# Adding both halves of every scan state to memory by accumulating transfers, in a decoder layer on one core

## The reference, cut to what matters

```python
def step(state, inp):
    d, b, c, u = inp
    dA = jnp.exp(d[..., None] * A)
    state = state * dA + (d * u)[..., None] * b[:, None, :]
    y = jnp.einsum('bdn,bn->bd', state, c)
    return (state, y)
...
y = y + D[None, :, None] * x
```

## Time and profile before

| | |
|---|---|
| median of 3 runs | 1617.96 us (1610.71 to 1623.04) |
| the profiled execution | 1609.87 us |
| its span in the profile | 1608.0 us |
| mean granted TensorE clock | 0.936 |
| TensorE busy | 1388.2 us (86%) |
| VectorE busy | 1288.5 us (80%) |
| GpSimd busy | 1137.2 us (71%) |
| ScalarE busy | 1044.1 us (65%) |

### The profile page before, as it was taken

One profiled execution on the slowest core, in us unless ns is written; L12 is line 12 of the kernel. 1 busy time (PEld: TensorE's weight loads), 2 busy tenths in 40 slices (PEclk: granted clock), 3 DMA queues, 4 the chain that ended last, 5 costly groups with the idle time before them and its releaser, 6 DMA issues.

```text
span 1608.0 us, 23140 instructions
## 1 busy us (share of the span) xinstructions
PE 1388.2 (86%) x7536; PEld 1130.4 (70%) x7536; DVE 1288.5 (80%) x2377; ACT 1044.1 (65%) x2411; POOL 1137.2 (71%) x613
## 2 busy tenths in 40 slices
PE   3645789998999999999989899985678998998996
PEld 1213678887878877878978788874456676776784
DVE  4898688998888898888898889897548577486575
ACT  3888366666666766666667667675457567577474
POOL 1345489888889888889988899998576266266263
PEclk8777889999999999999999999999689999999998
DMA  5485636656846666856676765657342122111021
GB/s 162 142 292 217 191 83 171 173 147 165 224 119 172 167 147 174 217 144 146 176 175 168 203 163 119 170 123 191 99 146 79 32 92 75 65 55 66 33 68 60
DMA packets 130314, 225.50 MB, mean 140 GB/s; under 512 B 11705, under 2 KB 61377, under 8 KB 128657
## 3 DMA queue, kind: packets, MB, share of 16 engines
q1 hardware_dynamic: 120400, 188.36, 36.9%
q0 software_dynamic: 9792, 35.66, 14.3%
HBM read 145.99 MB, written 77.99 MB: 139 GB/s over the span
## 4 chain that ended last, share of the span: by engine, by line
DVE 33%; PE 32%; issue 11%; ACT 10%; POOL 8%; DMA 5%; SPq 0%; DVEq 0%; POOLq 0%; ACTq 0%
PE banks L607 7%; PE banks L609 6%; PE banks L608 6%; DVE state L1175 5%; POOL act_buf L1974 5%; DVE negmax L1115 4%; PE banks L1514 3%; PE banks L1515 3%; PE banks L1516 3%; DVE prob L1129 2%; DMA x_lo<-scratch_xs 2%; ACT prob L944 2%; DVE banks L423 1%; DVE state_more L1175 1%; DVE qT_lo L1105 1%
## 5 line engine op out<-in xcount | busy, mean ns | idle before, releaser
L1306 POOL TENSOR_TENSOR state<-state,Cn 128x1024 f32<-128x1024 f32 x100 | 246.2, 2462 | 75.2 <-DVE state L1175 75.1
L1974 POOL TENSOR_TENSOR act_buf<-act_buf,wb 128x512 f32<-128x512 f32 x128 | 165.3, 1293 | 171.0 <-ACT act_buf L1873 169.2
L1281 POOL TENSOR_TENSOR state<-dtu_sb,Bn 128x1024 f32<-128x1024 f32 x103 | 249.6, 2424 | 21.6 <-DMA Bn<-scratch_bc 19.8
L1175 DVE TENSOR_TENSOR_SCAN state<-banks,state 128x512 f32<-128x512 f32 x206 | 249.8, 1213 | 2.6 <-ACT banks L998 2.0
L998 ACT ACTIVATE banks<-dt_sb,negA 128x512 f32<-128x512 f32 x256 | 177.3, 692 | 92.8 <-DVE state L1175 71.3
L607 PE MATMUL banks<-x_hi,w_hi 128*128 128x512 f32 (+1 forms) x512 | 187.3, 366 | 48.8 <-DVE qT_lo L1105 14.9
L609 PE MATMUL banks<-x_hi,w_lo 128*128 128x512 f32 (+1 forms) x512 | 178.7, 349 | 0.0
L608 PE MATMUL banks<-x_lo,w_hi 128*128 128x512 f32 (+1 forms) x512 | 178.5, 349 | 0.0
L607 PEld LDWEIGHTS banks<-x_hi,w_hi 128*128 128x128 f32 x512 | 101.9, 199 | 70.6 <-issue 26.1
L2022 DVE TENSOR_TENSOR hid_lo<-banks,hid_hi 128x512 fp32r<-128x512 f32 x136 | 93.7, 689 | 53.3 <-ACT hid_hi L1885 51.4
L2032 DVE TENSOR_TENSOR banks<-banks,act_buf 128x512 f32<-128x512 f32 x136 | 94.3, 693 | 49.0 <-POOL act_buf L1974 25.5
(11 more groups left out here) (226 smaller groups left out, 4587.4 us busy)
## 6 DMA issues: line engine op xcount, KB each, us to landing
scratch_y<-state POOLq DMA_DIRECT2D x52, 512.0 KB, 5.9
x_hi<-scratch_xs SPq DMA_DIRECT2D x32, 512.0 KB, 5.7
x_lo<-scratch_xs SPq DMA_DIRECT2D x32, 512.0 KB, 9.0
Cn<-scratch_bc SPq DMA_DIRECT2D x64, 256.0 KB, 3.7
Bn<-scratch_bc SPq DMA_DIRECT2D x64, 256.0 KB, 4.1
scratch_acc<-acc_sb SPq DMA_DIRECT2D x64, 256.0 KB, 2.2
wb<-scratch_wT SPq DMA_DIRECT2D x64, 256.0 KB, 3.3
acc_sb<-scratch_acc SPq DMA_DIRECT2D x48, 256.0 KB, 3.1
```

Source lines behind the costliest of these rows:

```text
L1175: nc.vector.tensor_tensor_scan(row, dA[:, :], row, 0.0, ALU.mult, ALU.add) \
L1281: nc.gpsimd.tensor_tensor(ring(k), dtu[:, 2 * h:2 * h + 2, :], Bn[:, state % NB, :].unsqueeze(1).broadcast_to([P, 2, T]), ALU.mult).then_i ...
L1306: nc.gpsimd.tensor_tensor(to, ring(k), Cn[:, state % NB, :].unsqueeze(1).broadcast_to([P, 2, T]), ALU.mult).then_inc(S["gated"], 1)
L1974: nc.gpsimd.tensor_tensor(act_[:, N % 3, :], act_[:, N % 3, :], wb[:, E % 3, :], ALU.mult) \
```

## The change

No half state is summed on chip any more. Every half state, h = 0 and h = 1, is gated in its ring buffer and added to memory by a transfer of its own. A transfer waits, on GpSimd, until the one before it to the same place has landed. The running sum y_sb goes; its room becomes a sixth buffer of the ring. A ring buffer comes free when its transfer has landed. The code that waits for the end of the sums is changed to match.

```diff
-RING = 5
+RING = 6
...
-    y = sb("y_sb", [P, 2, T])
-    st_more = sb("state_more", [P, 1, 2, T])
+    st_more = sb("state_more", [P, 2, 2, T])
...
-        def wait_free(k):
+        def wait_added(k):

             state, h = divmod(k, 2)
-            b, r = divmod(state, NS)
-            if h == 1:
-                pool.wait_ge(S[f"y_added1{state % 2}"], 16 * (state // 2 + 1))
-            elif r == 0:
-                pool.wait_ge(S["gated"], k + 1)
-            else:
-                pool.wait_ge(S["piece_done"], (NS - 1) * b + r)
+            pool.wait_ge(S[f"y_added{h}{state % 2}"], 16 * (state // 2 + 1))
...
             if k >= RING:
-                wait_free(k - RING)
+                wait_added(k - RING)
...
-            to = ring(k)
-            if h == 0 and r == 0:
-                if b > 0:
-                    pool.wait_ge(S["y_added0"], 16 * b)
-                to = y[:, :, :]
-            nc.gpsimd.tensor_tensor(to, ring(k),
+            nc.gpsimd.tensor_tensor(ring(k), ring(k),
                                     Cn[:, state % NB, :].unsqueeze(1).broadcast_to([P, 2, T]),
                                     ALU.mult).then_inc(S["gated"], 1)
-            if h == 0 and r > 0:
-                pool.wait_ge(S["gated"], k + 1)
-                nc.gpsimd.tensor_tensor(y[:, :, :], y[:, :, :], ring(k), ALU.add) \
-                    .then_inc(S["piece_done"], 1)
             if k + 3 < NDRIVE:
                 drive(k + 3)
-            if h == 1:
-                pool.wait_ge(S["gated"], k + 1)
-                if r > 0:
-                    wait_free(k - 2)
-                nc.gpsimd.dma_start(d["y"][b][:, 2 * T:4 * T],
-                                    ring(k).rearrange("p c t -> p (c t)"), accum_op=ALU.add) \
-                    .then_inc(S[f"y_added1{state % 2}"], 16)
-            elif r == NS - 1:
-                pool.wait_ge(S["piece_done"], (NS - 1) * (b + 1))
-                nc.gpsimd.dma_start(d["y"][b][:, 0:2 * T], y[:, :, :].rearrange("p c t -> p (c t)"),
-                                    accum_op=ALU.add).then_inc(S["y_added0"], 16)
+            pool.wait_ge(S["gated"], k + 1)
+            if r > 0:
+                wait_added(k - 2)
+            nc.gpsimd.dma_start(d["y"][b][:, 2 * h * T:2 * (h + 1) * T],
+                                ring(k).rearrange("p c t -> p (c t)"), accum_op=ALU.add) \
+                .then_inc(S[f"y_added{h}{state % 2}"], 16)
```

More of the change, by code:

```diff
@@ L596, in attend_and_scan @@
              "acc_loaded0", "acc_loaded1", "acc_stored0", "acc_stored1",
-             "dt_loaded0", "dt_loaded1", "dtu_loaded0", "dtu_loaded1", "y_added0", "y_added10", "y_added11",
+             "dt_loaded0", "dt_loaded1", "dtu_loaded0", "dtu_loaded1", "y_added00", "y_added01", "y_added10", "y_added11",
              "b_loaded0", "b_loaded1", "c_loaded0", "c_loaded1",
-             "dA_done", "dbu_done", "scan_done", "gated", "piece_done")
+             "dA_done", "dbu_done", "scan_done", "gated")
     S = {n: ctx.enter_context(nc.semaphore(n)) for n in names}
@@ L761, in sync @@
             sp.wait_ge(S[f"acc_stored{h}"], 16 * NM // 2)
-            sp.wait_ge(S[f"y_added1{h}"], 16 * NSTATE // 2)
-        sp.wait_ge(S["y_added0"], 16 * B)
+            for odd in range(2):
+                sp.wait_ge(S[f"y_added{h}{odd}"], 16 * NSTATE // 2)
     def tensor(pe, F, blocks=None):
@@ L1709, in first_loads @@
         sp.dma_start(rbias[:, :], d["route_b"].broadcast_to([P, NE])).then_inc(S["rows_loaded"], 16)
-        sp.wait_ge(A["y_added0"], 16)
-        for odd in range(2):
-            sp.wait_ge(A[f"y_added1{odd}"], 16 * NS // 2)
+        for h in range(2):
+            for odd in range(2):
+                sp.wait_ge(A[f"y_added{h}{odd}"], 16 * NS // 2)
         load_y(sp, 0)
@@ L1901, in scalar @@
         act.wait_ge(A["acc_done"], NM)
-        act.wait_ge(A["y_added0"], 16 * B)
         for n in range(2):
-            act.wait_ge(A[f"y_added1{n}"], 16 * NSTATE // 2)
+            for odd in range(2):
+                act.wait_ge(A[f"y_added{n}{odd}"], 16 * NSTATE // 2)
         for n in range(2):
```

## The result

The changed kernel takes 1626.99 us in the median of 20 runs (1617.66 to 1637.93), the kernel before 1615.82 us in 20 runs beside it. The ratio is 1.0067, with a 95% interval of 1.0052 to 1.0083: **10.8 us slower**.

A forecast was written before the change was run, and what follows sets the result against it. It took VectorE's and TensorE's own work and x's landing to bound the loop, not GpSimd. Terms 0 + 1 + 0 + 5 + 4 = +10 us on a median of 1618 gave 1628 us, range 1608 to 1648.

The forecast's parts named there:

- The sums go: 60 sums on GpSimd, 144 us, vanish; none is on the chain and nobody waits for them: 0 us.
- GpSimd turned up in the chain before 1100 us: Stated sign that the prediction is wrong: GpSimd appearing in the chain of waits before 1100 us.
- The issues, the ring and the waits for landings: On GpSimd, 53 us of issues fit the freed time; landing and buffer waits cost 0 while landings stay under some 13 us.
- Rival D: Landings beside x's load take over 13 us and stall GpSimd, then the scan: 30 us; chance 0.30 together with rival A.
- GpSimd's idle time before the gates: Sign of being right: GpSimd's idle time before L1306 much longer, its busy time near 1137 - 144 us.
- The holds: VectorE's `w_lo` and `ow_lo` locked out by GpSimd: the locks move, +2.7 us on VectorE, +1 us on the chain.
- x in items 2 and 3: In 8 items, the new transfer delays x's second half by 1.8 us and TensorE waits: +5 us.
- rival A: Transfers and x's loads share the engines in full, a late B sliding the transfer onto x: 1649 us; chance 0.30 with Rival D.
- x in the first item after a group's end: In 3 items, new transfers meet the store and x's second half: +1.3 us each, +4 us, bounds -3 and +10.
- a lower clock in the phase: Stated sign that the prediction is wrong: the granted clock in the attention and scan phase falls.
- The end: Last gate about 0.6 us sooner, but the chain into the experts goes by TensorE, VectorE and the attention sum's store: 0.
- Rival B: GpSimd's relief counts: VectorE's locks mostly vanish, up to 20 us faster, 1598 us (with half, 1608); chance 0.08.

The follow-up runs named there:

- f2: Kernel before with its 60 sums on chip done over 8 of 512 columns, the rest left out; ratio 0.9978 to the kernel before.
- f4: Changed kernel with the h = 0 transfers of states 1 to 11 (44 transfers) cut to 8 columns; ratio 1.0059 to the kernel before.
- f1: Kernel before with its four transfers of y_sb cut to 8 columns of 1024, sums on chip kept; ratio 0.9975 to the kernel before.
- f3: Changed kernel with the h = 0 transfers of states 0 and 12 to 15 (20 transfers) cut to 8 columns; ratio 0.9963 to the kernel before.
- e4: Changed kernel without h = 0 transfers, `w_lo` and `ow_lo` made with one SBUF operand (subtraction and factor left out); ratio 0.9740 to the kernel before.
- e3: Kernel before with `w_lo` and `ow_lo` made by a reduction with one SBUF operand (subtraction and factor left out); ratio 0.9800 to the kernel before.
- e1: Changed kernel without the transfers of h = 0, that part of the sum left out; 1606.43 us, ratio 0.9943 to the kernel before.
- g1: Changed kernel with each odd `w_lo` moved on VectorE from behind a step's scans to behind the next step's `turned_low`; ratio 0.9996 to the kernel before.

## Why the prediction was right, and where it was not

The median, 1627.0 us, is 1 us off the forecast. The sum came out (+10 against +10.8), but several of its terms did not: that it is so close is luck, since their errors cancelled. The terms below are read from the two profiled executions, which lie 16.5 us apart, where no run is named.

- **The sums go: 0. Measured -3.6** (f2, -0.3 to -6.8). I argued that nobody waits for GpSimd, and called the prediction wrong if GpSimd turned up in the chain before 1100 us. By that sign it is wrong: GpSimd is there after the change, between 921 and 1009 us, for instance with the gate at 933.15. It isn't what costs time, though, since nothing is lost in that stretch (the plateau of 13.9 us), and f2 has its gain with no GpSimd in its chain there. Where it comes from shows in part: f2 too has the freed `ow_lo` behind the groups' ends (TensorE's wait is 1.46 us there, and 3.54 before), while its `w_lo` costs 8.3 us more. I had both in the holds' term and put half on the path; behind the first two ends all of it was, behind the third almost nothing.
- **The issues, the ring and the waits for landings: 0.** Held in the loop. GpSimd waits for scratch_y once, 2.9 us at the very end, where it is in the chain. Rival D fell. GpSimd's idle time before the gates, of which I had said that it would be much longer, stayed (93.9 us for VectorE before, 94.8 after, with `state_more`): the freed time went into the waits for B. GpSimd's busy time is 1043.8 us, not 993: a gate takes 2598 ns instead of 2464 (128 x 0.134 = 17 us), and the rest is in smaller items.
- **The holds: +1 us, bounds -5 and +5.** The method was right for the five instructions that it looked at. I had forecast +0.9, +1.4, +1.3 and -0.3 us for four `w_lo` and -1.8 for one `ow_lo`; they became 1196 to 2530 ns, 2028 to 2774, 1211 to 2449, 2847 to 2533 and 2557 to 752. But a group has eight `w_lo`, and I had all of them with B on time. B was late (82.4 us of waits), GpSimd bunched, and two that had been free took 1810 and 1694 ns in the first group already. `w_lo` rose by 5.2, 4.3 and 7.0 us in the three groups, 16.5 in all (29.6 to 46.1, where `ow_lo` fell by 7.1), 5.3 us of it at one place. The steps with weight stages grew by 9.3 us and not by 16.5: TensorE's waits for x in the groups' last items shrank meanwhile, from 10.0 to 5.2 us; with the start (-2.8) and the steps behind the ends (-5.3) that leaves +1, as forecast, by other ways.
  The Trainium skill ("SBUF — State Buffer", SBUF: two separate sides) says that whichever instruction comes first has the shared ports for a whole instruction. The runs agree for one instruction, 2.5 us against 0.68; through three in a row one took 6.52 us.
- **x in items 2 and 3: +5. Measured +1.3 with all that lies in the middle** (f4, -2 to 5); the profile has +3.5, all in the first group. I had the wrong half. I took the first half to be safe by 1.8 us or more, but its x_lo now landed in 10.5 and 10.4 us, not 7.5 and 5.9, and TensorE waited for it (1.44 and 1.27 us). Of eight second halves one waited, 0.62 us. I had held GpSimd's schedule fixed and let the new transfer fall next to x. A late B made GpSimd's odd half late too, so the odd transfer, which had stood in the midst of x's load, moved towards its end. In the last such load, which ran from 1003.5 to 1017.7 before, it was issued 4.5 us after the start (1008.0). After, the load runs from 1017.6 to 1028.9; the new transfer goes out 2.8 us ahead of it (1014.8) and the odd one 7.1 us after its start (1024.7). The first x_lo takes 7.5 us there instead of 5.7, the second 7.5 instead of 10.2. x_lo lands in 8.6 us in the median, against 9.0; I had said 1 to 2 us longer. That also is why rival A (1649 us) did not come, though it named the same late B.
- **x in the first item after a group's end: +4, bounds -3 and +10. This is the step that failed.** The profile has +9.2 us in the three end steps (1.8, 2.9, 4.5), 3.1 an item where I took 1.3; of the 5.3 us given back behind them 2.5 are idle time, by the freed `ow_lo`, and 2.8 the clock. Two things were missing. The transfer delays not x alone but the store ahead of it in SyncE's chain, 7.1 us against 5.4. And the clock is lower behind the longer waits: in the second and third end TensorE is busy 1.8 and 1.5 us longer than before. I had no term for that, while the first end of the kernel before already had 0.67. My sign of being wrong, a lower clock in the phase, did not come, since the steps behind the ends and those of the last items had less of it: 0.98 before and 0.99 after.
- **The end: 0. Measured +1.2** at the 64th step, by the late load of the last C and the wait of 2.9 us, though f1 and f2 have 0.9 of it without new transfers. I had followed the attention's sum alone.

In runs: 12.8 us at the ends (16.8 of f3 less the 4.0 that y_sb's transfers cost there before), 1.3 in the middle and -3.6 by the relief make 10.5, against 10.8 measured. Rival B's premise, that relief is worth something, holds in a small size; rival A's, full contention everywhere, does not. The software queue's share was forecast at 45% and is 43.1%; the DMA share at 0.88, and is 0.82 in the stretch.

Open: how much of the relief's 3.6 us goes by `ow_lo`, since e4, without holds, is as far below e3 (9.7 us) as e1 is below the kernel before (9.2); what decides the long hold at the 45th step, which g1 has too and f3 and f4 don't; how the 16.8 us of f3 split between store, x, dt and dtu, and clock; and why the relief shows in f2's time and not in the span of its one profile (1608.3 us).

## What to carry to other kernels

A transfer's price isn't its share of the engines. Forty-four in the middle of the batches cost 1.3 us and twenty around their ends 16.8, and the traces show there a store, a reload and a load that TensorE waits for in one ordered queue: price added traffic by the chain that it meets, item by item, and move it to where nothing waits. Look what the clock does behind each stall that you lengthen, and then over the whole phase: here 3.5 us at the ends were made up for elsewhere. And don't hold the other engines' schedule fixed: the engine with slack slips first, and where it slips decides who is hit.

## What was unexpected of the hardware

- Removing the holds was worth more than the held time. In the kernel before `w_lo` and `ow_lo` lose 29.6 + 18.5 - 16.2 - 10.3 = 21.6 us of VectorE, and e3 is 32 us faster. TensorE's idle time before its matmuls on x fell from 30.4 to 12.7 us in it. Of that, the waits for `qT_lo` went from 14.9 to 6.3 us, and the three late landings of x in a group's last item (10.0 us) are gone: SyncE's weight stages wait for `w_lo`, and x stands behind them.
- The same two-operand instruction took 0.68, 2.5 and 6.52 us, by what GpSimd did beside it; with one operand in SBUF all 24 took 675 ns.
- The granted clock over the 4 us behind TensorE's waits of 3.0 to 3.3 us for x at the ends was 0.57 to 0.66; behind 0.86 and 1.66 us it was 1.00, behind 1.82 us 0.67, and behind a wait of 3.26 us for `qT_lo` (921.49, before) 1.00 again.
- An issue on GpSimd goes with a slower operation behind it: in the kernel after the 58 gates without one right ahead took 2.39 us in the mean and the 70 with one 2.77.
